# Two more products of a CIN tower made from fp32r halves: the chunk of two distances and the sum over d

## The reference

```
z1[p]  = x0[f] * x0[g]        for all f, g     x1 = z1 @ f0     (39*39  -> 128)
z2[p]  = x0[f] * x1[g]                         x2 = z2 @ f1     (39*128 -> 128)
z3[p]  = x0[f] * x2[g]                         x3 = z3 @ f2     (39*128 -> 128)
r1, r2, r3 = sums of x1, x2, x3 over d (16)
h = relu([r1, r2, r3, dense] @ W1 + b1);  h = relu(h @ W2 + b2);  y = h @ W3
```

## Time and profile before

| | |
|---|---|
| median of 3 runs | 1282.36 us (1281.91 to 1282.44) |
| the profiled execution | 1282.15 us, of which the span from first to last instruction is 1280.3 us |
| busy PE, DVE, POOL, ACT | 1247.0, 1038.5, 951.5, 751.1 us (97, 81, 74, 59% of the span) |
| TensorE clock granted | 1.000 |
| DMA | 78.69 MB, mean 61 GB/s |

### The profile page before, as it was taken

The page is one execution under the profiler, slowest core; times in us unless marked ns, Lnnn a source line. Parts: engine busy times, 40 slices in busy tenths (PEclk is TensorE's granted clock), DMA queues, the critical chain, the costliest instruction groups (busy, mean ns, idle before and its releaser), DMA issues.

```text
span 1280.3 us, 19891 instructions
## 1 busy us (share of the span) xinstructions
PE 1247.0 (97%) x5493; PEld 963.6 (75%) x5493; DVE 1038.5 (81%) x3346; ACT 751.1 (59%) x2422; POOL 951.5 (74%) x844
## 2 busy tenths in 40 slices
PE   1999999999999999999999999999999999999999
...
DMA packets 121764, 78.69 MB, mean 61 GB/s; under 512 B 77436, under 2 KB 89826, under 8 KB 121652
## 3 DMA queue, kind: packets, MB, share of 16 engines
...
## 4 chain that ended last, share of the span: by engine, by line
PE 97%; DMA 1%; POOL 1%; issue 0%; ACTq 0%; ACT 0%; DVE 0%; SPq 0%
PE ps L499 23%; PE ps L503 22%; PE ps L500 22%; PE ps L479 14%; PE ps L526 6%; PE ps L515 5%; PE ps L582 2%; PE ps L592 1%; PE ps L462 1%; POOL x_in L393 1%; DMA x_in<-in_tables,row_at 0%; PE ps L599 0%; ACTq L272 0%; DMA x_rows<-x_in 0%; DMA ids_now<-in_ids 0%
## 5 line engine op out<-in xcount | busy, mean ns | idle before, releaser
L823 DVE SCALAR_TENSOR_TENSOR terms<-ps,x_scal,terms 128x128 f32<-128x128 f32 x2944 | 805.7, 341 | 158.4 <-ACT terms L670 94.5
L670 ACT ACTIVATE terms<-ps,x_scal 128x128 f32<-128x128 f32 x2048 | 585.3, 369 | 370.4 <-PE ps L503 363.6
L417 POOL TENSOR_TENSOR terms<-terms 128x1024 f32<-128x1024 f32 (+2 forms) x384 | 577.4, 1504 | 178.5 <-DVE terms L823 156.3
L499 PE MATMUL ps<-w_high,x_high 128*128 128x512 f32 (+1 forms) x1280 | 581.7, 454 | 2.9 <-DVE x_low L801 2.9
L503 PE MATMUL ps<-w_high,x_low 128*128 128x512 f32 (+1 forms) x1280 | 496.1, 388 | 0.0
L500 PE MATMUL ps<-w_low,x_high 128*128 128x512 f32 (+1 forms) x1280 | 494.3, 386 | 0.0
L393 POOL DMA_INDIRECT x_in<-in_tables,row_at x320 | 305.2, 954 | 81.5 <-issue 65.1
L499 PEld LDWEIGHTS ps<-w_high,x_high 128*128 128x128 f32 x1280 | 240.6, 188 | 82.9 <-issue 20.6
L500 PEld LDWEIGHTS ps<-w_low,x_high 128*128 128x128 f32 x1280 | 241.1, 188 | 77.8 <-issue 29.8
L503 PEld LDWEIGHTS ps<-w_high,x_low 128*128 128x128 f32 x1280 | 240.1, 188 | 50.5
L479 PE MATMUL ps<-prods,w 117*128 117x512 f32 x262 | 136.1, 604 | 5.2 <-DVE prods L789 5.0
...
## 6 DMA issues: line engine op xcount, KB each, us to landing
...
x_in<-in_tables,row_at POOLq DMA_INDIRECT x320
x_diag<-x_scal SPq DMA_DIRECT2D x256, 9.8 KB
...
```

Source lines behind the costliest of these rows:

```text
L417: nc.gpsimd.tensor_tensor(t[:, 0:n], t[:, 0:n], t[:, n:2 * n], ALU.add).then_inc(s_tree, 1)
L499: nc.tensor.matmul(y, x1_high[:, par, at:at + P], high, start=True, stop=False)
L670: op = nc.scalar.activation(terms[:, u % 2, FB * ACT_BANKS.index(q) + i, :], ps[:, (BANKS * u + q) % RING, i * G:(i + 1) * G], ACT.Copy, s ...
L823: nc.vector.scalar_tensor_tensor(out=acc, in0=y, scalar=x0, in1=acc, op0=ALU.mult, op1=ALU.add).then_inc(s_mac, 1)
```

## The change

- **Chunk of two distances.** The chunk with two distances (78 rows) becomes chunk 1 and is called `REST`; the others are renumbered (`SHIFT_OF`), and `SPLIT` is 2, 3 and 4. The spare 39 rows of the contraction hold low halves: ACT makes the high half of the 78 product rows in `rest`, DVE the low half in `prods_low`, and ACT issues two DMAs (`move_rest`) that bring the first and then the second 39 low rows under the 78 high ones. PE makes two passes of fp32r, at (1, 3) with the weights' high half and at (2, 1) with the low half. The old fp32 matmul of it is gone; `cin1` has 8 slots in place of 7.
- **Sum over d.** `x2` is split as well: ACT makes the high half at q 6 of the step after (`split_x2_high`), DVE the low half at q 7 (`split_x2_low`), and POOL writes the next x2 but one only when the low half is there. The scalars are split once in a group (`x0_hl`; ACT at (0, 4), DVE at (0, 5)), and the 8 DMAs of `move_diag` copy both halves. PE makes three fp32r passes of 320 columns.
- **Waits.** `sum_s3` waits for both halves of x2. Before it writes `x0_hl`, ACT waits until the former group's `x0_diag` has landed (`guard`). At the start, two DMAs for `w0_rest` come ahead of the last moves and of `put_diag(0)` in SP's list.
- **Order.** One product moves from (2, 3) to (2, 1), and a fourth high and low are added at (2, 2) and (2, 3). `dense_rows` shares memory with `r2`. In the tail, the dense weights are split ahead of the store of s3.

```diff
...
-SPLIT = (1, 2, 3)
+SHIFT_OF = (0, KT - 1) + tuple(range(1, KT - 1))
+REST, SPLIT = 1, (2, 3, 4)
 NS = len(SPLIT)
+KH = (SPT - 1) * F
...
-PRODUCTS = ((0, 2), (0, 4), (1, 2), (1, 7), (2, 3), (2, 5), (2, 7))
-HIGHS = ((0, 6), (1, 4), (1, 8))
-LOWS = ((0, 7), (1, 5), (1, 9))
-CIN1 = ((0, 6), (1, 1), (1, 8), (2, 6), (2, 9), (3, 2), (3, 4))
+X2_HIGH, X2_LOW = 6, 7
+SPLIT_SCALARS = (0, 5)
+PRODUCTS = ((0, 2), (0, 4), (1, 2), (1, 7), (2, 1), (2, 5), (2, 7))
+HIGHS = ((0, 6), (1, 4), (1, 8), (2, 2))
+LOWS = ((0, 7), (1, 5), (1, 9), (2, 3))
+MOVE_LOWS = ((0, 8), (1, 3))
+CIN1 = ((0, 6), (1, 3), (1, 8), (2, 1), (2, 6), (2, 9), (3, 2), (3, 4))
+CIN1_OF = (0, REST, 2, REST, 3, 4, 5, 6)
+SLOTS = len(CIN1)
+REST_SLOTS = tuple(n for n, k in enumerate(CIN1_OF) if k == REST)
...
@@ -145,12 +154,17 @@
         prods = sb("prods", [P, KT, GCOLS])
         prods_high = sb("prods_high", [KR, NS, GCOLS], F32R)
         prods_low = sb("prods_low", [KR, NS, GCOLS], F32R)
+        rest = sb("rest", [KR, GCOLS], F32R)
+        w0_rest = sb("w0_rest", [KR, 2, G], F32R)
         x1_high = sb("x1_high", [P, 2, GCOLS], F32R)
         x1_low = sb("x1_low", [P, 2, GCOLS], F32R)
         x0_scal = sb("x0_scal", [P, 2, TILES, F])
-        x0_diag = sb("x0_diag", [P, 2, TILES, TB, FX])
+        x0_hl = sb("x0_hl", [P, 2, TILES, F], F32R)
+        x0_diag = sb("x0_diag", [P, 2, 2, TILES, TB, FX], F32R)
         terms = sb("terms", [P, 2, TERMS, G])
         x2 = sb("x2", [P, 2, G])
+        x2_high = sb("x2_high", [P, G], F32R)
+        x2_low = sb("x2_low", [P, G], F32R)
...
-        dense_rows = sb("dense_rows", [P, NBATCH, ROWS3])
...
+        dense_rows = r2[:, 0:NBATCH * ROWS3].rearrange("p (c k) -> p c k", k=ROWS3)
...
         def move_second(queue, k, j):
             at = j % GROUPS * GCOLS
-            queue.dma_start(prods[0:KR, k, :], x0_cols[k:k + KR, at:at + GCOLS]).then_inc(s_second[k - 1], 16)
+            row, n = SHIFT_OF[k], KH if k == REST else KR
+            queue.dma_start(prods[0:n, k, :], x0_cols[row:row + n, at:at + GCOLS]).then_inc(s_second[k - 1], 16)
+
+        def move_rest(queue, i):
+
+            queue.dma_start(rest[KH:KR, :].bitcast(F32), prods_low[i * F:(i + 1) * F, 0, :].bitcast(F32)) \
+                .then_inc(s_rest, 16)
...
+            def put_diag(j):
+
+                for b in range(TB):
+                    at = slice(b * D, (b + 1) * D)
+                    sp.dma_start(x0_diag[at, j % 2, :, :, b, 0:F].bitcast(F32), x0_hl[at, :, :, :].bitcast(F32)) \
+                        .then_inc(s_diag[j % 2], 16)
+
             def move_diag(gf, j):
-                sp.wait_ge(s_scal, gf + 1)
+                sp.wait_ge(s_scl, gf + 1)
                 sp.wait_ge(s_s3, gf * TILES - TILES + CREDIT_S3)
-                for b in range(TB):
-                    rows = slice(b * D, (b + 1) * D)
-                    sp.dma_start(x0_diag[rows, j % 2, :, b, 0:F], x0_scal[rows, j % 2, :, :]) \
-                        .then_inc(s_diag[j % 2], 16)
+                put_diag(j)
             def move_seconds(gf, j):
-                for k in range(1, KT):
-                    sp.wait_ge(s_cin1, gf * KT - KT + k + 1)
-                    move_second(sp, k, j)
+                for n in range(1, SLOTS):
+                    sp.wait_ge(s_cin1, gf * SLOTS - SLOTS + n + 1)
+                    if n != REST_SLOTS[0 if gf == 1 else 1]:
+                        move_second(sp, CIN1_OF[n], j)
             def next_cols(gf, j):
...
+                    .then_inc(s_wrest, 16)
             move_seconds(1, 1)
-            sp.wait_ge(s_ones, 1)
-            sp.wait_ge(s_scal, 1)
-            for b in range(TB):
-                rows_b = slice(b * D, (b + 1) * D)
-                sp.dma_start(x0_diag[rows_b, 0, :, b, 0:F], x0_scal[rows_b, 0, :, :]).then_inc(s_diag[0], 16)
+            sp.wait_ge(s_ones, 2)
+            sp.wait_ge(s_scl, 1)
+            put_diag(0)
             load_late()
             for j in range(1, GROUPS + 1):
                 feed(0, j)
@@ -417,7 +450,8 @@
                     nc.gpsimd.tensor_tensor(t[:, 0:n], t[:, 0:n], t[:, n:2 * n], ALU.add).then_inc(s_tree, 1)
                 pool.wait_ge(s_tree, bt * (STEPS * len(TREE)) + len(TREE) * (u + 1))
-                pool.wait_ge(s_s3, bt * STEPS + u - 1 + CREDIT_S3)
+                if bt * STEPS + u > 1:
+                    pool.wait_ge(s_x2l, bt * STEPS + u - 1)
                 nc.gpsimd.tensor_tensor(x2[:, u % 2], t[:, 0], t[:, 1], ALU.add).then_inc(s_x2, 1)
...
+                if k == REST and first:
+                    pe.wait_ge(s_prod, k + 1)
+                    cols = slice(half * 256, half * 256 + 256)
+                    passes = ((w0[0:KH, k, :], prods[0:KH, k, cols]),)
+                elif k == REST:
+                    pe.wait_ge(s_wrest, 32)
+                    pe.wait_ge(s_rest, (gf - 1) * 32 + half * 16 + 16)
+                    passes = ((w0_rest[:, half, :], rest[:, :]),)
+                elif k in SPLIT and not first:
                     i = SPLIT.index(k)
-                    pe.wait_ge(s_low, gf * NS - NS + i + 1)
+                    pe.wait_ge(s_low, (gf - 1) * (NS + 1) + i + 2)
+                    low = prods_low[:, (i + 1) % NS, :]
                     passes = ((w0_high[:, i, :], prods_high[:, i, :]), (w0_low[:, i, :], prods_high[:, i, :]),
-                              (w0_high[:, i, :], prods_low[:, i, :]))
+                              (w0_high[:, i, :], low))
                 else:
                     pe.wait_ge(s_prod, gf * KT + k + 1)
                     passes = ((w0[:, k, :], prods[0:KR, k, :]),)
-                for n, (w, x) in enumerate(passes):
-                    mm = nc.tensor.matmul(ps[:, X1_BANK, :], w, x, start=(k == 0 and n == 0),
-                                          stop=(k == KT - 1 and n == len(passes) - 1))
+                for i, (w, x) in enumerate(passes):
+                    mm = nc.tensor.matmul(ps[:, X1_BANK, cols], w, x, start=(k == 0 and i == 0),
+                                          stop=(n == SLOTS - 1 and i == len(passes) - 1))
                 mm.then_inc(s_cin1, 1)
             def cin2(bt, u, q, scalars_next):
...
+                pe.wait_ge(s_x2h, bt * STEPS + u - 1)
+                pe.wait_ge(s_x2l, bt * STEPS + u - 1)
                 j, t = divmod(u - 2, TILES)
                 if t == 0:
...
-                                 x0_diag[:, j % 2, t].rearrange("p b f -> p (b f)"),
-                                 start=True, stop=True).then_inc(s_s3, 1)
+                s3_sum = ps[:, S3_BANK, 0:TB * FX]
+                high, low = (x0_diag[:, j % 2, i, t].rearrange("p b f -> p (b f)") for i in range(2))
+                nc.tensor.matmul(s3_sum, x2_high[:, :], high, start=True, stop=False)
+                nc.tensor.matmul(s3_sum, x2_high[:, :], low, start=False, stop=False)
+                nc.tensor.matmul(s3_sum, x2_low[:, :], high, start=False, stop=True).then_inc(s_s3, 1)
             def cin3(bt, lo, hi):
...
@@ -637,9 +685,12 @@
                     act.wait_ge(s_mac, gf * (TILES * MACS) - TILES * MACS + CREDIT_MAC)
                     if j > 1:
                         act.wait_ge(s_s3, gf * TILES - 2 * TILES + 1 + CREDIT_S3)
-                nc.scalar.activation(x0_scal[:, j % 2, :, :],
-                                     ps[:, X1_BANK, 0:TILES * F].rearrange("p (t f) -> p t f", f=F),
-                                     ACT.Copy).then_inc(s_scal, 1)
+                turned = ps[:, X1_BANK, 0:TILES * F].rearrange("p (t f) -> p t f", f=F)
+                if guard:
+                    before = gf - 1
+                    act.wait_ge(s_diag[before % 2], (before // 2 + 1) * (16 * TB))
+                nc.scalar.activation(x0_hl[:, 0, :, :], turned, ACT.Copy).then_inc(s_sch, 1)
+                nc.scalar.activation(x0_scal[:, j % 2, :, :], turned, ACT.Copy).then_inc(s_scal, 1)
             def store_first(bt, j):
...
+                if k == REST:
+                    act.wait_ge(s_cin1, (gf - 1) * SLOTS + REST_SLOTS[1] + 1)
+                    nc.scalar.activation(rest[0:KH, :], prods[0:KH, k, :], ACT.Copy).then_inc(s_high, 1)
+                else:
+                    nc.scalar.activation(prods_high[:, i - 1, :], prods[0:KR, k, :], ACT.Copy).then_inc(s_high, 1)
             def store_x1(gf, j):
...
+
+            def split_x2_high(bt, u):
+
+                act.wait_ge(s_x2, bt * STEPS + u + CREDIT_X2)
+                act.wait_ge(s_s3, bt * STEPS + u - 1 + CREDIT_S3)
+                nc.scalar.activation(x2_high[:, :], x2[:, (u - 1) % 2, :], ACT.Copy).then_inc(s_x2h, 1)
...
                     if q in ACT_BANKS:
                         scale(bt, u, q)
+                    if q == X2_HIGH and bt + u > 0:
+                        split_x2_high(bt, u)
                     if front and now == FIRST_AT:
                         store_first(bt, j)
                     if q == S3_AT + 1 and u >= 2:
...
                         split_high(gf, HIGHS.index(now))
```

(41 more changed lines are left out.)

58 lines of the change are left out of this document (37 added, 21 removed).

## The result

The changed kernel takes 1345.01 us (median of 4 runs, 1342.66 to 1348.09) against 1282.13 for the kernel before beside it (1281.51 to 1282.44): a ratio of 1.0493, with a 95% interval from 1.0481 to 1.0505. I had forecast 1298 and a range up to 1311. The sign was right; three quarters of the loss were not in my sum. The profiled execution has a span of 1340.9 us, 60.5 more than before.

A forecast was written before the change was run, and what follows sets the result against it. PE, with 97% of the chain of waits, was taken to bound the kernel before. 1282.15 - 23.9 (PE's gain) + 31.8 (waits at (1, 3)) + 6.0 (start) + 1.8 (tail) = 1297.9, forecast as 1298; range 1268 to 1311.

The forecast's parts named there:

- PE's prices: PE's matmul costs: 0.23 a pass, 0.15 for 320 columns; chunk gains 12.4 us, sum over d 11.5, together 23.9.
- The turns: Intervals between POOL's starts of adds, tiles 0 to 3: 9.3, 9.0, 9.7, 7.8; 35.8 a group against PE's 34.52.
- The start: PE's first cin1 of group 1 comes 6.0 us late, since ACT waits for put_diag(0) to land.
- The tail: Last four steps: a PE step takes 7.2, the loop of POOL, ACT and DVE 7.8; 1.8 us over three turns.
- Where the lag is paid: PE waits at (1, 3) for the moved lows, 0.3 plus a lag growing 1.28 a group; 31.8 us in all.
- The loop: POOL, ACT and DVE waiting on each other through x2 and its halves; one group takes 35.8 us (35.3 to 36.3).
- After each batch's cin3 the lag starts from nothing: POOL's 6.44 us wait behind each batch's cin3 clears the lag, which then grows 1.28 a group.
- PE stays the bound: Rival, 24%: turns are shorter than added up and PE's five banks take the rest; 1276, or 1266 without waits at (1, 3).
- The moved lows are late: Rival, 8%: a DMA queued behind SP's makes PE wait 1.3 at (1, 3) in each group, 40 us; 1307.
- my own case: Main case, 50%: the loop of POOL, ACT and DVE outlasts PE's group and PE idles at (1, 3); 1298 us.

The follow-up runs named there:

- chunk_29: The chunk's edit alone against the kernel before, with the new low half at (2, 9) and its chunk taken last: 1279.68 us, ratio 0.9980.
- all_edits: Changed kernel with x2's halves at q 8 and 9, s3 stored first, row_at doubled, separate group 0 halves, fourth low at (2, 9), late weights after first feed: 1281.26 us.
- s3_first: The changed kernel, but at q 6 ACT stores s3 before it waits for x2 and makes its high half: 1318.78 us, ratio 1.0287.
- rows_twice: The changed kernel with two copies of the row numbers, so POOL numbers behind tile 2's gathers without waiting for the last gather: 1331.77 us, ratio 1.0382.

## Why the prediction was right and wrong

- **PE's prices: right one by one, less so in sum.** 0.23 a pass; 0.14 to 0.15 for 320 columns, where I took 0.15. The chunk's gain is 0.36 a group in chunk_29, where I had 0.40. The group of a PE that nothing holds is 34.79 in all_edits against 34.52: of the 0.76 that I had a group gain, 0.49 came. Where the other 0.27 are is open.
- **The turns: right.** Tiles 0 to 3 forecast at 9.3, 9.0, 9.7 and 7.8, measured 9.18, 8.84, 10.06 and 7.81; the sum 35.89 against 35.8. That the sum is so close is partly luck, as tile 2 was 0.36 too low and tiles 0 and 1 were 0.28 too high. The low half at (2, 3) took 1.61 where I had 1.5 for one that meets an add. I had taken 9.7 for tile 2 between that and none; the rule of the Trainium skill, SBUF — State Buffer, "SBUF: two separate sides", would have made it 10.2, and the trace is with the rule (10.06).
- **The start: right in size.** 6.0 forecast, 5.84 measured, by the mechanism named. The issue did not follow the bytes (5.44).
- **The tail: right.** 7.8 a turn forecast, 7.82 measured.
- **Where the lag is paid: wrong in the place.** I had PE idle at (1, 3), growing from group to group. PE waits for the moved lows there for 6.4 us in the whole run, at most 1.9; the larger waits are for banks, behind DVE's MACs (19.6, and 41.6 for its weight loads). POOL's waits in tile 2's turn did not vanish either (0.70 before 746.19). The loop closes through PE's banks, not only through POOL.
- **"After each batch's cin3 the lag starts from nothing": this step failed.** I had a batch at 4 x 34.52 + 9.0 + 4.1 = 151.2; it took 156.7. I had taken the 6.44 that POOL waits behind `cin3` as slack for the loop. It is none, since `cin3` doesn't start at PE's own pace: it needs the last s3, which ACT stores behind x2's half, which waits for POOL. So the lag stands in front of `cin3` and `cin3` comes on top. By terms: 1.0 for a group's lag that is not given back, 1.9 for the wait, 1.6 for the clock in five of seven, 2.05 for the numbering, less the 1.25 of these that is not paid and not explained, and 0.4 for the turns; 5.7 against the 5.5 that are missing. Of the 45 us that I was short, the six full batches are 33. The first batch lost 9.5 where I had 1.1 for a batch, 8 more, and the rest is in the last.
- **What was in my text for it.** I had written that the store of s3 is queued behind the wait for x2, and priced it only as 0.42 in tile 0's turn; I didn't ask who waits for that store. And I counted POOL's adds, x2 and gathers in its list, and not the numbering, which the trace of before has once a batch with a wait of 1.51 ahead of it (690.03). s3_first and rows_twice put 26.2 and 13.2 on those two. Of the 26.2, some 8 to 9 are tile 0's shorter turns (0.31 by 28 groups), which I had priced; the rest, 17 to 18, and the 13 of the numbering I had not.
- **The rivals.** "PE stays the bound" is what all_edits and chunk_29 become, not this kernel. "The moved lows are late" was nearer in time (1307) than my own case, still 38 short, and its mechanism is not this kernel's: PE waits for the moved lows 6.4 in all, where that rival had 40.

A cause only argued, not shown: that the clock fell because PE had been half idle. s3_first takes wait and fall away together, but at 21 of the 42 borders with the wait it was there without the fall.
